# Expert weights split in place during the attention; the token table uses their memory first

## The chip, the cores and the metric

The kernel runs on one core of a Trainium2 chip. A core has TensorE (PE), VectorE (DVE), ScalarE (ACT), GpSimd (POOL) and SyncE (SP, which here only starts DMAs), and 16 DMA engines. Each engine runs its own list of instructions in order, and they wait for each other by semaphores. The metric is the device time in microseconds (us) of one execution.

## The reference

4096 tokens (16 sequences of 256) go through an embedding, six layers of linear attention and a mixture of experts. Width D is 256.

```python
h = take(W.T, x)                          # W: [256, 50257], ids below 12564
a = layernorm(h)
for l in range(6):
    t = layernorm(a) * gamma[l] + beta[l]
    q, k, v = split(t @ w_qkv[l])
    q = softmax(q, axis=1); k = softmax(k, axis=2)
    out = einsum('bic,bij->bjc', q, einsum('bic,bjc->bij', k, v))
    a = a + out @ w_out[l] + b_out[l]
h = h + a
x = layernorm(h)
# 8 experts, top 2 of x @ gate_w, weights by softmax of the two; and one shared expert
h = h + sum_e w_e * ((silu(x @ w1[e]) * (x @ w2[e])) @ w3[e]) + shared(x)
```

## The kernel before

Every product is made in float16 with each factor split in a high and a low part (high times high, high times low, low times high), so each weight is needed as two float16 tiles: high is the float32 value scaled by 64 and rounded, low is the difference that rounding left. An expert has 3072 float32 columns (w1 and w2 side by side, then w3); there are nine experts with the shared one.

Stages, in order of time:

1. **Table.** The ids need only the first columns of W, which lie the wrong way round. SP loads chunks of 512 columns into `VW` (four buffers), TensorE transposes them, ScalarE and VectorE copy one half each from PSUM to `VR`, ScalarE's queue stores them as rows to `emb_rows` in DRAM. A stretch is 7 steps of 4 chunks, 28 chunks; with these ids there is one stretch. SP loads the weights of experts 0 and 1 ahead of the first chunk and of 2 and 3 behind it, into two float32 buffers `FST` (1.57 MB an expert); `expert_high` (L911, L912, ScalarE) and `expert_low` (L1087, L1089, VectorE) split them.
2. **Gathers.** When all rows are stored, GpSimd issues 32 indirect DMAs (L544) into `X`. In this time SP loads the other five experts and the two engines split all that are left.
3. **First norm.** Per group of 8 tiles (four groups): VectorE takes statistics (L1116, L1119), GpSimd adds epsilon and takes the root (L566, L568), SP stores the gathered rows as `h0_rows` (L383) for a later addition, VectorE normalizes `X` in place (L1128) once store and root are done. GpSimd's `cut` (L561) makes the low parts of layer 0's weights between its roots; ScalarE makes the high ones (L941, L945). SP waits until all experts are split before it stages layer 0's weights.
4. **Attention.** 96 items (16 sequences, 6 layers), one turn each, as a software pipeline written out in `item_loop`. In turn t TensorE works at q and k of item t+2 and at m, p and the output of item t; VectorE normalizes item t+5 (L1156) and takes statistics of item t+6; GpSimd does gamma and beta, the bias and the split of item t+5 (L579 to L592) and the root of item t+6 (L596). VectorE and GpSimd start at turn -6 (`AHEAD`), the others at -2: turns -6 to -1 are called lead turns here. SP issues the transposes of h (L423) and of the exponent of q (L432). The turns of the first half of each layer (`prep`) also split a slice of the next layer's weights: ScalarE scales and rounds, GpSimd takes the difference (`cut`). ScalarE and GpSimd have nested loops for this, VectorE and TensorE one plain loop over pairs of turns.
5. **Feed-forward.** Gates, ranks, scattering of tokens to slots, the shared expert (16 pairs of tiles) and 39 pairs of slots of the eight experts. For each pair TensorE does two `up` halves (L809, 24 multiplies each) and a `down` (L825, 24). Which expert's weights a pair takes is read from a table, so the columns of these weights have a register in their address (`cols`, `which`).

Orders that matter for the change. VectorE in a turn: reciprocal of k's sums (L1169), the addition of item t-1 (L1163), low v (L1174), low m (L1178), maximum of q (L1183), maximum of k (L1186), low k (L1190), norm (L1156), low PR (L1196), statistics (L1200), low exponent of q (L1207), aggregates (L1213). TensorE's last four multiplies of an item (L759) wait for the low PR; the products m, q, k, p, v (L712) follow, twelve multiplies each. ScalarE in a turn: high v (L983), high m (L989), high k (L995), negated maximum of q (L999), exponents (L1004, L1009), high PR (L1014), exponents of k.

Of the kernel before, what the change touches and what calls it, by code (L numbers as in the profile page):

```python
# [17 lines left out]
def tower(nc, x_ids, tok_w, w_qkv, w_out, b_out, gamma, beta, gate_w, ew1, ew2, ew3, sw1, sw2, sw3, out):  # L18
# [37 lines left out]
    VBUF = 4  # L56
    VSTEP = VCH * VBUF
    VBLK = VCH // P
    STRETCH = 7
    VROWS = STRETCH * VSTEP  # L60
    NSTRETCH = -(-VOCAB // VROWS)
# [17 lines left out]
    with ctx:  # L79
# [8 lines left out]
        W12h = sb("W12h", [P, NE, KH, 2 * HID], f16)  # L88
        W12l = sb("W12l", [P, NE, KH, 2 * HID], f16)
        W3h = sb("W3h", [P, NE, HC, D], f16)  # L90
        W3l = sb("W3l", [P, NE, HC, D], f16)
# [11 lines left out]
        padt = sb("padt", [P, 2, ROW], f32)  # L103
# [17 lines left out]
        s_fstage = [sem(f"s_fstage{i}") for i in range(2)]  # L121
        s_fhi, s_flo = sem("s_fhi"), sem("s_flo")
        s_gath = [sem(f"s_gath{i}") for i in range(4)]
        s_h0st = [sem(f"s_h0st{i}") for i in range(4)]
        s_reuse, s_passed, s_passed_sp = sem("s_reuse"), sem("s_passed"), sem("s_passed_sp")
# [3 lines left out]
        NG4 = NT // 4  # L129

        emb = ExitStack()
        ident = sb("ident", [P, P], f32, emb)
        VW = [sb(f"VW{i}", [P, KH, VCH], f32, emb) for i in range(VBUF)]
        VR = [h0b[:, 0, :, :], h0b[:, 1, :, :]]
        VR += [sb(f"VR{i}", [P, VBLK, D], f32, emb) for i in range(2, VBUF)]
        FST = [sb(f"FST{i}", [P, KH * 2 * HID + HC * D], f32, emb) for i in range(2)]  # L140

        idrow = W3l[0:1, :, :, :].rearrange("p e c n -> p (e c n)").bitcast(i32)[:, 0:TOK]
        idmax = sb("idmax", [1, 1], i32, emb)
        emb.close()

        FW12 = KH * 2 * HID


# [7 lines left out]
        WSN = WL // WSL  # L156
        Wsc = sb("Wsc", [P, WSN], f32, att)
        Wn = sb("Wn", [P, 2, WL], f16, att)
        hhl = [sb(f"hhl{i}", [P, 2, TB, D], f16, att) for i in range(2)]
        rows = sb("rows", [P, 2, 3, D], f32, att)  # L160
# [16 lines left out]
        att.close()  # L177

# [128 lines left out]
        def item_loop(eng, one, lead, prepare=False, behind={}):  # L307

            def pair(h, prep):
                for p in range(2):  # L310
                    one(eng.snap(h * 2 + p), p, prep)

            for t in range(-lead, 2):
                one(t, t % 2, prepare and t >= 0)
            if not prepare:
                with eng.Fori(1, (ITEMS - AHEAD) // 2) as h:
                    pair(h, False)
# [12 lines left out]
            for t in range(ITEMS - AHEAD, ITEMS):  # L330
                one(t, t % 2, False)
                if t in behind:
                    behind[t]()
# [1068 lines left out]
```

## Time and profile before

| | us |
|---|---|
| median of 3 runs | 1513.89 |
| lowest and highest | 1504.29, 1516.38 |
| the profiled execution | 1518.33 |
| its span, first to last instruction | 1516.6 |

The engines' busy time in the stages of the profiled execution:

| stretch, us | what | PE | DVE | ACT | POOL | granted PE clock | DMA, GB/s |
|---|---|---|---|---|---|---|---|
| 0 to 96 | table | 43.92 | 30.26 | 23.95 | 2.31 | 0.75 | 365 |
| 96 to 154 | gathers | 0.00 | 30.52 | 19.64 | 42.35 | 0.50 | 276 |
| 154 to 195 | first norm, lead turns | 0.59 | 23.63 | 6.88 | 25.27 | 0.50 | 132 |
| 195 to 985 | attention | 765.67 | 680.29 | 596.48 | 685.07 | 0.99 | 79 |
| 985 to 1130 | attention's end, gates, shared expert | 117.48 | 81.24 | 75.44 | 81.41 | 0.94 | 113 |
| 1130 to 1517 | shared expert, experts | 355.48 | 182.51 | 109.31 | 135.47 | 0.98 | 64 |

How to read rows: a line of the timeline gives the start, the duration, the engine, the line in the code, the operation, what it writes and reads, the shape and the count; in brackets stands how long the engine had been idle and what ended that. Rows of the same kind that follow each other are merged, so a duration with x8 is that of eight instructions. Matmuls overlap, so their rows are longer than their distance. PEld is TensorE's load of weights. The clock is a share of 2.4 GHz.

### The profile page before, as it was taken

What the parts mean: (1) busy time and instruction counts of PE and PEld (TensorE: products, weight loads), DVE (VectorE), ACT (ScalarE), POOL (GpSimd) and SP (SyncE); (2) the same over time, 40 slices, a digit from 0 to 9 for tenths busy, and PEclk for the clock granted to TensorE, in tenths of its full rate; (3) what the DMA queues carried; (4) which work ended last, traced back from release to release, by engine and by line L of the source; (5) the groups of instructions that cost most, each with busy time, mean ns of one, the idle gap of its engine ahead of it and who ended that gap; (6) DMA issues with size and microseconds to landing.
All of it is one profiled execution on the core that took longest, in us unless ns stands there. A gap on an engine that the chain in (4) does not pass through costs nothing. (4 is left out here: it accounts for less than half of the span.)

```text
span 1516.6 us, 37800 instructions
## 1 busy us (share of the span) xinstructions
PE 1283.1 (85%) x11400; PEld 1096.8 (72%) x11401; DVE 1028.5 (68%) x2634; ACT 831.7 (55%) x2253; POOL 971.9 (64%) x967
## 2 busy tenths in 40 slices
PE   2620069999999999999999999877898999999996
PEld 2520058888888888888888888766787888888885
DVE  3235558888888888888888888765456444444443
ACT  2233148777877777787787777665442222222231
POOL 0037589888988988988888888647542333333333
PEclk8755589999999999999999999999999999999998
DMA  9998433253235235333523423684434343434340
GB/s 321 398 323 299 129 69 63 62 128 69 62 69 128 62 64 127 69 62 76 121 59 66 97 61 64 92 113 126 113 99 134 64 65 53 69 54 69 51 69 8
DMA packets 356716, 160.28 MB, mean 106 GB/s; under 512 B 283953, under 2 KB 340273, under 8 KB 356657
## 3 DMA queue, kind: packets, MB, share of 16 engines
q1 hardware_dynamic: 321810, 119.56, 33.7%
q0 software_dynamic: 20064, 25.32, 9.0%
q10 hardware_dynamic: 14784, 14.68, 2.7%
q8 instruction: 29, 0.48, 0.1%
q14 instruction: 29, 0.24, 0.0%
HBM read 46.08 MB, written 44.21 MB: 60 GB/s over the span
## 5 line engine op out<-in xcount | busy, mean ns | idle before, releaser
L712 PE MATMUL bank<-hT,Wc 128*128 128x256 f16 x2304 | 286.3, 275 | 110.5 <-DMA hT<-hhl 104.9
L712 PEld LDWEIGHTS bank<-hT,Wc 128*128 128x128 f16 x2304 | 226.8, 99 | 138.9 <-issue 111.3
L674 POOL DMA_INDIRECT out_rows<-h0b,payin x78 | 121.7, 1560 | 232.6 <-DVE h0b L1370 203.8
L809 PE MATMUL bank<-xTg,W12h 128*128 128x256 f16 x1248 | 187.2, 273 | 0.0
L579 POOL TENSOR_TENSOR h0b<-h0b,rows 128x512 f32<-128x512 f32 x96 | 122.0, 1270 | 94.0 <-issue 47.3
L1038 ACT ACTIVATE silu<-bank 128x512 f32<-128x512 f32 x110 | 65.5, 596 | 211.0 <-PE bank L809 205.2
L1311 DVE SCALAR_TENSOR_TENSOR gT<-bank,silu 128x512 f32<-128x512 f32 x110 | 76.0, 691 | 144.4 <-ACT silu L1038 142.0
L712 PE MATMUL bank<-Wc,MT 128*128 128x256 f16 x1152 | 142.3, 274 | 8.6 <-DVE MT L1178 8.6
L825 PE MATMUL bank<-W3h,gThl 128*128 (+1 forms) x880 | 127.5, 276 | 23.5 <-DVE gThl L1317 20.5
L712 PE MATMUL bank<-khl,eqT 128*128 128x256 f16 x1152 | 141.4, 272 | 5.7 <-issue 0.2
L712 PE MATMUL bank<-Wc,hT 128*128 128x256 f16 x1152 | 141.7, 273 | 0.0
L809 PEld LDWEIGHTS bank<-xTg,W12h 128*128 x1248 | 122.1, 98 | 14.2
L712 PEld LDWEIGHTS bank<-khl,eqT 128*128 128x128 f16 x1152 | 109.7, 98 | 28.9 <-issue 16.5
L1317 DVE TENSOR_TENSOR gThl<-gT,gThl 128x512 f16<-128x512 f32 x110 | 76.6, 696 | 78.1 <-ACT gThl L1042 73.1
L712 PEld LDWEIGHTS bank<-Wc,MT 128*128 128x128 f16 x1152 | 112.6, 98 | 23.1 <-DVE MT L1178 9.7
L1042 ACT ACTIVATE gThl<-gT 128x512 f16<-128x512 f32 x110 | 69.3, 630 | 98.2 <-DVE gT L1311 94.4
L1156 DVE TENSOR_SCALAR h0b<-X,amv,arstd 128x256 f32 (+1 forms) x192 | 79.1, 453 | 64.8 <-POOL arstd L596 64.8
L712 PEld LDWEIGHTS bank<-Wc,hT 128*128 128x128 f16 x1152 | 112.9, 98 | 13.3
L585 POOL TENSOR_TENSOR hhl<-h0b,rows 128x512 f16<-128x512 f32 x96 | 122.1, 1272 | 0.0
L586 POOL TENSOR_TENSOR h0b<-h0b,rows 128x512 f32<-128x512 f32 x96 | 122.0, 1270 | 0.0
L580 POOL TENSOR_TENSOR X<-X,rows (+2 forms) x96 | 121.9, 1270 | 0.0
L825 PEld LDWEIGHTS bank<-W3h,gThl 128*128 128x128 f16 x880 | 85.1, 98 | 49.2 <-issue 31.1
(153 smaller groups left out, 2941.3 us busy)
## 6 DMA issues: line engine op xcount, KB each, us to landing
VW<-in_L_tok_W SPq DMA_DIRECT2D x28, 512.0 KB, 6.3
FST<-in_L_ffn_ew SPq DMA_DIRECT2D x24, 512.0 KB
emb_rows<-h0b ACTq DMA_DIRECT2D x14, 512.0 KB, 8.2
emb_rows<-VR ACTq DMA_DIRECT2D x14, 512.0 KB, 9.4
Wc<-Wn SPq DMA_DIRECT2D x48, 128.0 KB, 2.2
Wst<-in_L_attn_w_qkv SPq DMA_DIRECT2D x6, 768.0 KB, 4.8
h_rows<-X SPq DMA_DIRECT2D x4, 1024.0 KB, 4.5
X<-h_rows POOLq DMA_DIRECT2D x8, 512.0 KB, 6.9
```

Source lines behind the costliest of these rows:

```text
L579: pool.tensor_tensor(xn[:, :, :], xn[:, :, :], row(0), ALU.mult).then_inc(s_hg, 1)
L580: pool.tensor_tensor(tiles(u), tiles(u), row(2), ALU.add).then_inc(s_xb, 1)
L585: pool.tensor_tensor(h_hi, xn[:, :, :], row(1), ALU.add)
L586: pool.tensor_tensor(hf[:, :, :], xn[:, :, :], row(1), ALU.add).then_inc(s_hf, 1)
L674: pool.indirect_dma_start(out=out_rows, out_offset=bass.IndirectOffsetOnAxis(ap=got(j % PAYS, w, 0, i32), axis=0), in_=yout[j % 2][:, w, : ...
L712: last = mm(to, lhs(a, k, o), moving, start=(i == 0 and k == 0), stop=(i == 2 and k == 1))
L809: last = mm(to, cols((W12h, W12l)[a], e, k, w * HID + (2 * half + c) * P, P), moving, start=(n_ == 0), stop=(n_ == 5))
L825: last = mm(pb[4 + p][:, w * D:(w + 1) * D], gThl[:, p, a, c, w * P:(w + 1) * P], cols((W3h, W3l)[b], e, c, 0, D), start=(n_ == 0), stop=( ...
L1042: A(gThl[:, p, 0, 2 * half:2 * half + 2, :], gT32[:, half, :, :], ACT.Copy).then_inc(s_ghi, 1)
L1156: last = V.tensor_scalar(xn[:, k, :], X[:, bass.ds(seq(w) * TB + k, 1), :].rearrange("p a n -> p (a n)"), amv[p][:, k, 0:1], arstd[p][:, k ...
L1311: V.scalar_tensor_tensor(gT32[:, half, :, :], pb[2 * half + 1][:, :].rearrange("p (c n) -> p c n", c=2), 1.0 / WS, silu[:, half, :, :], AL ...
L1317: V.tensor_tensor(gThl[:, p, 1, c, :], gT32[:, half, :, :], gThl[:, p, 0, c, :], ALU.subtract).then_inc(s_glo, 1)
```

## The change

- The nine experts' high and low parts are one float16 tile `Wall` (9 x 6144 columns), high and low alternating in chunks of 512 columns, 54 chunks in all. The same memory, seen as float32 (`Wf`), first holds the table's buffers, now five of each kind (`VBUF = 5`, a stretch is 5 steps of 5 chunks: 25 chunks), the ids, the identity, and the gathered rows `G`.
- Experts are loaded as float32 into `Wf`, one expert's width ahead of where their parts go, and split in place, one copy (ScalarE) and one difference (VectorE) of 512 columns a turn: 8 chunks ahead of the attention, 8 in the second half of each of the first five layers, the last 6 in turns 84 to 89. The shared expert comes into a buffer of its own (`lastf`) that overlays attention weights no longer needed.
- Experts 0 and 1 are loaded when the table is stored, 2 and 3 between the transposes of items 1 and 2, four more at the end of a layer each, the last at the start of the last layer.
- Rows are gathered into `G`, and the norm goes from `G` to `X`, so it does not wait for the store of `h0_rows`.
- Layer 0's weights are staged right behind the table's loads; their low parts are taken by VectorE. Only the first of GpSimd's four roots and of VectorE's four norms stands ahead of the lead turns: the other roots follow turns -6, -5, -4, the other norms turns -5, -3, -1.
- VectorE takes the nested loops too. The padding row is stored from one tile by a broadcast.

```diff
-    VBUF = 4
+    VBUF = 5
+    EXP = KH * 2 * HID + HC * D
+    XCH = HID
+    XPER = EXP // XCH
+    XALL = NE * XPER
+    XEARLY = NB // 2
-    STRETCH = 7
+    STRETCH = 5
...
+        PLAIN, CUT, EXPERT, LAST = range(4)
+        def item_loop(eng, one, lead, other=True, between={}):
...
+                with eng.Fori(1, quarter) as h:
+                    pair(h, CUT)
+                with eng.Fori(0, quarter) as b:
+                    pair(eng.snap(b + quarter), EXPERT, eng.snap(b + XEARLY // 2))
                 with eng.Fori(1, DEPTH - 1) as l:
+                    with eng.Fori(0, quarter) as b:
+                        pair(eng.snap(l * (2 * quarter) + b), CUT)
+                    with eng.Fori(0, quarter) as b:
+                        pair(eng.snap(l * (2 * quarter) + b + quarter), EXPERT, eng.snap(l * quarter + b + XEARLY // 2))
...
@@ sync
+            n = steps(sp)
+            with sp.Fori(1, n) as step:
...
+            stage(0)
+            stage_rows(0)
...
+            for j in range(VBUF):
+                sp.wait_ge(s_wst[j], n * 16)
+            for e in range(2):
+                load_expert(e)
             for j in range(4):
                 install(0, j)
             stage(1)
...
             turns(-4, 0)
             turns(-3, 1)
+            for e in range(2, 4):
+                load_expert(e)
+            stage_rows(1)
...
                     stage(l + 2)
                     stage_rows(l + 2)
+                if l + 4 < E:
+                    sp.wait_ge(s_xlo, NB // 2 * l + XEARLY + 1)
+                    load_expert(l + 4)
@@ gpsimd
+            first_root(0)
...
+            item_loop(pool, one, AHEAD, between={g - 7: partial(first_root, g) for g in range(1, 4)})
@@ tensor
+            def cols(a, e, chunk, c0, n):
+
+                return Wall[:, bass.ds(e * 2 * EXP + (chunk * 2 + a) * XCH + c0, n)] if isinstance(e, int) else \
+                    Wall[:, bass.ds(e + ((chunk * 2 + a) * XCH + c0), n)]
@@ scalar, def one, behind the high part of k
+                if c is not None:
+                    act.wait_ge(s_xload, 48 * (NE if kind == LAST else layer(t) + 4))
+                    act.sem_inc(s_passed, 1)
+                    act.wait_ge(s_xlo, c)
+                    act.sem_inc(s_passed, 1)
+                    expert_high(c, staged_last(c) if kind == LAST else staged(c))
@@ vector
+            def expert_low(n, from_):
+
+                dve.wait_ge(s_xhi, n + 1)
+                V.scalar_tensor_tensor(Wall[:, bass.ds(n * (2 * XCH) + XCH, XCH)], from_, WS,
+                                       Wall[:, bass.ds(n * (2 * XCH), XCH)], ALU.mult, ALU.subtract).then_inc(s_xlo, 1)
...
+            def first_norm(g):
                 dve.wait_ge(s_rstd, g + 1)
                 for t in range(8 * g, 8 * g + 8):
+                    last = V.tensor_scalar(X[:, t, :], G[:, t, :], mv[:, t, 0:1], rstd[:, t:t + 1], ALU.subtract, ALU.mult)
...
+            for n_ in range(XEARLY):
+                expert_low(n_, staged(n_))
...
+            for g in range(4):
+                first_stats(g)
+            first_norm(0)
...
                     last.then_inc(s_klo, 1)
+                if c is not None:
+                    expert_low(c, staged_last(c) if kind == LAST else staged(c))
                 if have(t + 5):
                     norm(t + 5, 1 - p)
...
+            item_loop(dve, one, AHEAD, between={**{2 * g - 7: partial(first_norm, g) for g in range(1, 4)},
+                                                **{ITEMS - 5 + g: partial(stats_of, g) for g in range(5)}})
```

## Rows read from the trace of the kernel before

**Rows 1.** Stretch, length; busy PE, PEld, DVE, ACT, POOL; clock, DMA share, GB/s.
```profile
625.00:697.00 72.00, 70.62 (x633) 60.40 (x632) 62.92 (x156) 57.17 (x182) 64.18 (x69) 1.00 0.30 62
```

**Rows 2.** Same columns, ten microseconds of the table phase.
```profile
74.00:84.00 10.00, 5.90 (x25) 4.79 (x26) 2.77 (x4) 2.39 (x4) 0.00 (x0) 0.53 1.07 396
```

**Rows 3.** Timeline (start us, us, engine, line, operation [idle before]) of the gathers.
```profile
99.65 2.50 POOL L544 DMA_INDIRECT X<-emb_rows,idx  x1 [96.32 <-issue]
...
112.23 2.29 DVE L1087 SCALAR_TENSOR_TENSOR W12l<-FST,W12h 128x2048 f16<-128x2048 f32 x1 [6.74 <-ACT W3h L912]
...
113.45 1.95 POOL L544 DMA_INDIRECT X<-emb_rows,idx  x1 [0.30 <-issue]
...
149.87 1.01 POOL L544 DMA_INDIRECT X<-emb_rows,idx  x1 [0.30 <-issue]
```

**Rows 4.** Timeline, from the last gather to the first attention turn.
```profile
153.02 0.32 POOL L552 TENSOR_SCALAR idx<-idx 128x32 int32<-128x32 int32 x1 [2.14 <-DMA X<-emb_rows,idx]
...
155.87 2.67 DVE L1128 TENSOR_SCALAR X<-X,mv,rstd 128x256 f32<-128x256 f32 x8 [4.52 <-POOL rstd L568]
...
158.46 2.70 DVE L1116 BATCH_NORM_STATS2 stats<-X 128x6 f32<-128x256 f32 x8
...
175.45 3.29 DVE L1128 TENSOR_SCALAR X<-X,mv,rstd 128x256 f32<-128x256 f32 x8 [3.08 <-POOL rstd L568]
...
179.81 0.76 DVE L1200 BATCH_NORM_STATS2 stats<-X 128x6 f32<-128x256 f32 x2
```

**Rows 5.** Timeline, GpSimd in two lead turns, and the first maximum of q.
```profile
182.84 1.26 POOL L579 TENSOR_TENSOR h0b<-h0b,rows 128x512 f32<-128x512 f32 x1 [0.94 <-issue]
...
190.62 1.26 POOL L579 TENSOR_TENSOR h0b<-h0b,rows 128x512 f32<-128x512 f32 x1 [0.94 <-issue]
...
199.11 0.66 DVE L1183 TENSOR_REDUCE qmax<-bank 128x2 f32<-128x512 f32 x1
```

**Rows 6.** Timeline of one turn in the middle of the attention.
```profile
553.86 0.20 ACT L999 ACTIVATE nqmax<-qmax 128x2 f32<-128x2 f32 x1 [0.81 <-DVE qmax L1183]
...
554.71 0.87 DVE L1190 SCALAR_TENSOR_TENSOR khl<-bank,rzks,khl 128x256 f16<-128x256 f32 x2
...
555.35 0.71 POOL L596 TENSOR_TENSOR arstd<-avar,mhalf 128x2 f32<-128x2 f32 x1
...
556.09 0.74 DVE L1156 TENSOR_SCALAR h0b<-X,amv,arstd 128x256 f32 x2 [0.51 <-POOL arstd L596]
...
556.74 0.69 DVE L1196 SCALAR_TENSOR_TENSOR PR<-bank,PR 128x512 f16<-128x512 f32 x1
...
557.48 0.61 PE L759 MATMUL bank<-PR,vT 128*128 128x256 f16 x4
...
559.54 1.47 PE L712 MATMUL bank<-hT,Wc 128*128 128x256 f16 x12
...
560.85 1.47 PE L712 MATMUL bank<-Wc,hT 128*128 128x256 f16 x12
```

**Rows 7.** Timeline of the feed-forward, VectorE's difference beside GpSimd's.
```profile
1101.84 0.69 DVE L1317 TENSOR_TENSOR gThl<-gT,gThl 128x512 f16<-128x512 f32 x1 [0.70 <-ACT gThl L1042]
...
1104.95 2.13 POOL L627 TENSOR_TENSOR xrow<-h0b,xrow 128x1024 f16<-128x1024 f32 x1 [4.65 <-ACT xrow L976]
...
1106.77 0.85 DVE L1317 TENSOR_TENSOR gThl<-gT,gThl 128x512 f16<-128x512 f32 x1 [0.69 <-ACT gThl L1042]
```

**Rows 8.** Timeline, maxima of q in every second turn, fourth layer.
```profile
659.63 0.68 DVE L1183 TENSOR_REDUCE qmax<-bank 128x2 f32<-128x512 f32 x1
...
676.24 0.68 DVE L1183 TENSOR_REDUCE qmax<-bank 128x2 f32<-128x512 f32 x1
...
692.47 0.68 DVE L1183 TENSOR_REDUCE qmax<-bank 128x2 f32<-128x512 f32 x1
```

**Rows 9.** Timeline, TensorE in a down product of the feed-forward.
```profile
1298.36 0.65 PE L825 MATMUL bank<-W3h,gThl 128*128 x4 [0.39 <-DVE gThl L1317]
...
1298.85 0.60 PE L825 MATMUL bank<-W3l,gThl 128*128 x4
```

More of the change, by code:

```diff
@@ L305, in tower, with pair, hook @@
         AHEAD = 6
-        def item_loop(eng, one, lead, prepare=False, behind={}):
-            def pair(h, prep):
+        PLAIN, CUT, EXPERT, LAST = range(4)
+        def item_loop(eng, one, lead, other=True, between={}):
+            def pair(h, kind, c=None):
                 for p in range(2):
-                    one(eng.snap(h * 2 + p), p, prep)
+                    one(eng.snap(h * 2 + p), p, kind, None if c is None else eng.snap(c * 2 + p))
+            def hook(t):
+                if t in between:
+                    between[t]()
+            quarter = NB // 4
@@ L439, in turns @@
                     turn_eq(t + 2 if isinstance(t, int) else sp.snap(t + 2), p)
-            stage(0)
-            stage_rows(0)
+            for j in range(VBUF):
+                sp.wait_ge(s_wst[j], n * 16)
+            for e in range(2):
+                load_expert(e)
             for j in range(4):
@@ L542, in _ @@
                 pool.sem_inc(s_passed, 1)
[L543 to L547 removed]
+                for g in range(4):
+                    gather(g)
                 for g in range(4):
@@ L715, in _, with one @@
             blk = lambda o: slice(o * P, (o + 1) * P)
-            def one(t, p, prep):
+            def one(t, p, kind, c):
                 u = t + 2
@@ L1025, in one @@
                     A(zks[:, :], zk[:, :], ACT.Copy, scale=1.0 / KS).then_inc(s_zks, 1)
-                if prep:
+                if kind == CUT:
                     l = layer(t) + 1
                     cut(t + WSL if isinstance(t, int) else act.snap(WSL * l + t % WSL), l, t % WSL)
-            item_loop(act, one, 2, prepare=True, behind={ITEMS - 4: lambda: high(0), ITEMS - 2: lambda: high(1)})
+            item_loop(act, one, 2, between={ITEMS - 4: lambda: high(0), ITEMS - 2: lambda: high(1)})
             def gate(i, p, half):
@@ L1140, in _ @@
             dve.wait_ge(s_route, 2)
+            for g in range(4):
+                first_stats(g)
+            first_norm(0)
             def stats_of(g):
@@ L1214, in one @@
                     last.then_inc(s_amv, 1)
-            item_loop(dve, one, AHEAD, behind={ITEMS - 5 + g: partial(stats_of, g) for g in range(5)})
+            item_loop(dve, one, AHEAD, between={**{2 * g - 7: partial(first_norm, g) for g in range(1, 4)},
+                                                **{ITEMS - 5 + g: partial(stats_of, g) for g in range(5)}})
             add(ITEMS - 1)
```

250 lines of the change are left out of this document (110 added, 140 removed).

## The prediction, made before the change was run

> **What bounds the kernel now.** I read the stage table first (busy time by stretches), then ten-microsecond stretches of the table phase, then the timeline of the gathers, of the stretch up to the first attention turn, and of one turn in the middle of the attention.
>
> From 195 us on TensorE is the bound: in a steady attention stretch it is busy 70.6 of 72 us at a granted clock of 1.00 (2.4 GHz) [rows 1]. Up to 195 us nothing is bound by compute. First the table phase: 28 chunks of 512 columns go in and out (2 x 0.524 MB each) and four experts' weights are loaded beside them; the DMA engines are full at 396 GB/s [rows 2]. Then 32 gathers are issued by GpSimd from 99.65 to 150.88 us, one per 1.31 us (1.01 and 0.30 idle) where nothing disturbs them [rows 3]. Then, from 153.02 to 179.81 us, four groups of root, norm and weight cut run one after another before the first attention turn starts its statistics [rows 4]. From that mark the rest is one chain, so a microsecond saved before it is saved at the end.
>
> **The change, part by part.**
>
> *Table phase.* Before: 28 chunks are 29.4 MB, twelve expert arrays of 0.524 MB are 6.3 MB. After: stretches of 5 steps of 5 chunks, 25 chunks, 26.2 MB, no expert. 9.4 MB less at 396 GB/s [rows 2] is 23.8 us. I give back 2 us, an estimate: the five first loads land together, and a new load waits for a transpose, so the queues run dry once near 10 us. Gathers start at 99.65 - 21.8 = 77.9. Bounds: 17 to 24 us.
>
> *Gathers.* They take 51.2 us against 32 x 1.31 = 41.9. The other 9.3 us is stalls of this kind: the 2.29 us difference of 2048 elements runs on VectorE from 112.23 to 114.52, and the gather begun at 113.45 ends at 115.40, which is 0.88 after the difference ended [rows 3]. Seven such pairs of differences (2.29 and 1.22 us) stand in this stretch, so 38% of their time became stall. After, eight expert differences of 0.69 [rows 7] and eight small cuts of about 0.35 fall here: 8.3 us, of which 30% is 2.5. Gathers take 44.4, 6.8 less. Bounds 41.9 and 50.2. The Trainium skill (SBUF — State Buffer, Who interferes with whom) says that a VectorE instruction with two SBUF inputs contends with a GpSimd one that reads SBUF, and that descriptor writing needs the other half of the port. The rows do not contradict it if it is the gather's start, which reads indices, that waits; if nothing waited, the gathers would take 41.9 and the sum would be 2.5 us lower.
>
> *Roots, norms and cuts.* Layer 0's cuts move to VectorE under the gathers, where it waits anyway, as do the early eight expert chunks on ScalarE and VectorE. The norm no longer waits for the store of h0. After the last gather only two things remain ahead of turn -6: statistics of the last group (2.70 and about 0.7 for its aggregates) and the norm of the first (2.67), 6.1 us; the root (153.02 to 155.87) runs beside the statistics [rows 4]. 26.8 becomes 6.1: -20.7.
>
> Mark of the first turn: 179.81 - 21.8 - 6.8 - 20.7 = 130.5, -49.3.
>
> *Lead turns.* Three roots (about 2.0 us each: 0.3 and 1.7 within the 2.85 of [rows 4]) now stand on GpSimd behind turns -6, -5, -4. GpSimd paces these turns, 7.78 us from one to the next, and idles 0.94 in each for the norm [rows 5], so a root costs 2.0 - 0.94, three 3.2. Norms of groups 1 to 3 (24 instructions of about 0.33) stand on VectorE among GpSimd's 1.27 us operations. How they collide shows in the old norms: 2.67 where GpSimd worked at a root, 3.29 beside a cut [rows 4]. I take 3 us (bounds 0 and 24 x 0.33 = 8). Experts 2 and 3 are loaded in SP's queue between the transposes of items 1 and 2: 3.1 MB at 396 GB/s is 7.9 us in a turn of about 8.8; 1 us. Queued behind it are the first transposes of h and of q, which TensorE waits for. Together +7.
>
> *Expert chunks in 46 turns* (40 in second halves of layers, 6 in the last). ScalarE's copy, about 0.6 us, is put ahead of the negated maximum, where it idles 0.81 [rows 6]: nothing, but it would cost up to 0.6 without that gap. VectorE's difference is 0.69 undisturbed [rows 7], between the low part of k and the norm. There the low part ends at 555.58 and the norm starts at 556.09, since GpSimd's root ends at 556.06 [rows 6]: 0.51 of cover. With 0.69 and one more wait (0.05, estimated) the norm starts 0.23 later. Behind it stand the low part of PR (556.74 to 557.43) and TensorE's four multiplies that wait for it (557.48), then m, q and k, whose maximum and low part lead back to the norm. This ring has no other slack, so each turn is 0.23 longer: 46 x 0.23 = +10.6. Bounds: 0 (all in the idle time) and 0.69 x 46 = 32.
>
> *Nested loops on VectorE.* It takes the nested loops that ScalarE and GpSimd already had. A pair of turns with cuts takes 16.61, one without 16.23 [rows 8], so extra sequencer work costs tenths at most; VectorE's own hides behind its 0.69 and 0.24 us operations at the turn's end. 0, bound 40 pairs x 0.38 = 15.
>
> *Expert loads in the layers* (five of 1.57 MB, four of them behind the weight stage, at 396 GB/s 4.0 us of DMA each [rows 2]). The next transposes queue behind them; TensorE uses those nearly a turn later. +1, bound 5 x 4 = 20.
>
> *Feed-forward.* Same multiplies, but twice as many register offsets, since high and low parts alternate in one tile. At a down product, four multiplies with new offsets take 0.65 where four with old ones take 0.60 [rows 9]. Four more such in each of 39 pairs: 39 x 0.05 = +2, bound 5.
>
> **Sum.** -49.3 + 7 + 10.6 + 0 + 1 + 2 = -28.7. The span 1516.6 becomes 1487.9. The profiled execution took 1518.3, 4.4 above the median of 1513.89; against the median the sum gives 1485.2.
>
> **Rivals.**
>
> *A. As summed*, within some 10 us: 1485.
>
> *B. TensorE hides it all.* Its own work in a turn is 7.86 us (72 multiplies of 0.109; the twelve multiplies of one product start 1.31 apart), under the 8.1 of the steady turn. If the 10.6 vanishes and the lead turns cost 3: 1513.9 - 49.3 + 3 + 3 = 1470.6. Against it: the ring above, where TensorE already waits for PR's low part.
>
> *C. The difference isn't covered at all.* VectorE reads both inputs from SBUF, as in the feed-forward, where such a difference takes 0.69 alone and 0.85 when begun 0.31 before the end of a GpSimd operation [rows 7]: it waits for that operation. In the turn it meets GpSimd's root, which ends at 556.06 [rows 6]. Then the norm starts at 556.06 + 0.69, 0.66 late: 46 x 0.66 = 30.4 instead of 10.6, 1513.9 - 28.7 + 19.8 = 1505, within 1%. For it: 0.85. Against: a root of 1.7 us did not lengthen the eight norms beside it (2.67) [rows 4]. The Trainium skill (SBUF — State Buffer, Who interferes with whom) has this as an exclusive lock for the whole instruction; by that rule this case holds.
>
> *D. The table phase is bound by its buffers' round trip, not by bytes.* Then 3 chunks of about 3.0 us and the 7 us of experts ahead of the first chunk go, 16 instead of 21.8: 1491. Against it: the DMA engines' busy share of 1.07 at 396 GB/s [rows 2].
>
> *E. Slower.* The difference arrives in the turn while GpSimd's longer operation (1.16 to 1.27 us) runs, waits for its end, and pushes back the next one on GpSimd, whose root the norm needs. One such meeting costs up to 1.27 + 0.69 - 0.51 = 1.45 per turn, 46 x 1.45 = 67: 1513.9 - 39.3 + 67 = 1541. It turns the sign from 39.3 / 46 = 0.85 us per turn. Against it: the norm holds GpSimd back in every turn, so GpSimd is at its root or idle when the difference comes [rows 6].
>
> **Chances.** A 0.60, B 0.10, C 0.17, D 0.08, E 0.05. I take 1% (15 us) as about what a measurement of this kernel can tell from no change. A, B, D are faster by more than that: 0.78. C falls within 1% with most of its chance: 0.16. Slower: 0.06. The time is that of A, 1485; the range runs from 1467 (B, with the gathers at their floor) to 1504 (next to C).
>
> **What the profile after would show.** Gathers start near 78, end near 122; the first turn's statistics near 130; the first maximum of q near 152 (199.11 before [rows 5]); pairs of turns with expert chunks near 16.7 against 16.23, pairs with cuts as before at 16.6; feed-forward longer by 2. Wrong would be: a gather start above 84 (D), pairs with expert chunks at 17.5 (C) or above 18 (E), VectorE's difference longer than 0.7 in those turns, or more than 12 us lost between the first maximum of q and turn 0.

## The result, and the profile after

| | before | after |
|---|---|---|
| median of 20 runs each, us | 1509.65 (1504.29 to 1516.38) | 1504.12 (1499.55 to 1509.61) |
| ratio | | 0.996, 95% interval 0.9945 to 0.9975 |
| the profiled execution, us | 1518.33, span 1516.6 | 1501.22, span 1499.3 |

The change brings 5.5 us, 0.4%, where 29 were forecast (a ratio of 0.981). It is less than the 1% that the prediction took as no change, and 1504.12 stands just past the upper end of the range, 1504, where rival C was expected; but C is not what happened.

The same marks in both profiles tell where the time went. "q(n)" is the start of the maximum of q of item n, so six layers are q(0) to q(95). "First gate" is ScalarE's table load ahead of its first silu, and "thirtieth half" is its thirtieth silu; the shared expert has 32 of them.

| us | before | after | difference | forecast |
|---|---|---|---|---|
| gathers start | 99.6 | 81.3 | -18.3 | -21.8 |
| first gather to first statistics of turn -6 | 80.2 | 50.5 | -29.7 | -27.5 |
| from there to q(0) | 19.3 | 29.0 | +9.7 | lead turns, in all +7 |
| layer 0, q(0) to q(16) | 132.6 | 135.1 | +2.5 | chunks +1.8, part of the lead turns |
| layers 1 to 4, q(16) to q(80) | 524.2 | 550.0 | +25.8 | chunks +7.4, loads +1 |
| layer 5, q(80) to q(95) | 126.5 | 128.5 | +2.0 | chunks +1.4 |
| q(95) to the first gate | 20.6 | 20.9 | +0.3 | 0 |
| gates and shared expert, to the thirtieth half | 157.8 | 146.2 | -11.6 | 0 |
| from there to the end | 355.8 | 357.8 | +2.0 | +2 |

The differences add up to -17.3, the difference of the two spans. The medians differ by 5.5 only. The row of -11.6 fits this gap: the change alters nothing in that stretch but the addresses of its weights, and over all kernels of this document it takes from 146 to 161 us (below). The profiled execution of before, 8.7 above its median of 20, had it long; that of after, 2.9 under its median, had it short. Without it -5.7 is left.

One row spoils the forecast: layers 1 to 4. Their turns are alike (7.9 to 8.6 us from one maximum of q to the next) but for one in each layer, the second, which takes 14.09, 15.28, 14.51 and 14.16 us after and 8.23 to 8.26 before. These four are +25.0. Some of it comes back two turns later (8.09 to 8.11 us where before has 8.60 to 8.61), and a kernel without the long turns (the first experiment) takes 527.7 us for the four layers. So the long turns cost 22.3 of the 25.8, net, and the chunks 3.5.

Stretches of the profile after, in the form of [rows 1]: the steady attention is as before, 70.64 us of TensorE in 72. The second fence has the turn before a long one, the first 14.1 us of the long one of layer 2 (it runs from 441.40 to 456.68), and the 8 us behind those.

```profile
core 0: us, PE busy (x) PEld busy (x) DVE busy (x) ACT busy (x) POOL busy (x), PEclk, DMA share, GB/s
625.00:697.00 72.00, 70.64 (x632) 60.41 (x630) 65.38 (x160) 58.05 (x183) 63.01 (x67) 1.00 0.32 62
```

```profile
433.40:441.40 8.00, 8.00 (x75) 6.97 (x74) 7.61 (x21) 6.48 (x21) 6.54 (x8) 1.00 0.73 201
441.40:455.50 14.10, 9.33 (x64) 7.20 (x62) 7.16 (x18) 5.36 (x18) 9.86 (x11) 0.76 0.75 204
455.50:463.50 8.00, 8.00 (x76) 7.15 (x74) 6.96 (x18) 6.69 (x22) 3.43 (x3) 1.00 0.18 35
```

TensorE, VectorE and ScalarE each do about one turn's work in nearly twice the time, so it is a wait for something else. The timeline of that turn after (SPq are SP's DMA issues):

```profile
435.55 0.43 SPq L390 DMA_DIRECT2D Wall<-in_L_ffn_ew  x1
436.02 0.47 SPq L391 DMA_DIRECT2D Wall<-in_L_ffn_ew  x1
436.89 1.80 SPq L392 DMA_DIRECT2D Wall<-in_L_ffn_ew  x1
438.89 3.36 SPq L414 DMA_TRANSPOSE hT<-hhl  x1
442.44 3.76 SPq L423 DMA_TRANSPOSE eqT<-EQhl  x1
448.24 0.84 ACT L1031 ACTIVATE EQhl<-bank,nqmax 128x256 f16<-128x256 f32 x2 [4.87 <-DMA eqT<-EQhl]
449.60 0.69 DVE L1227 SCALAR_TENSOR_TENSOR PR<-bank,PR 128x512 f16<-128x512 f32 x1 [4.45 <-ACT PR L1036]
449.71 1.87 PE L766 MATMUL bank<-PR,vT 128*128 128x256 f16 x8 [4.77 <-ACT PR L1036]
452.22 2.76 PE L722 MATMUL bank<-khl,eqT 128*128 128x256 f16 x12
```

And the DMA issues of 438.5 to 443.2 in the same trace, us from issue to landing in the last column:

```profile
hT<-hhl SPq DMA_TRANSPOSE x1, 8.4
eqT<-EQhl SPq DMA_TRANSPOSE x1, 5.8
```

The reader is to see a chain. From 432.93 SP issues the next layer's weight stage (1.4 MB) and right behind it the expert's 1.57 MB. The transposes stand behind those 3 MB: the issue of one takes 3.36 and 3.76 us instead of 1.24, and the landing of h's 8.4 instead of 3.1. `EQhl` has one buffer, so ScalarE may not write the next exponent before the transpose has read the last; it stands 4.87 us at L1031. The high part of PR, its next instruction, is late, and VectorE and TensorE wait 4.45 and 4.77 for it. Then the granted clock has fallen: the stretch has 0.76, and eight multiplies take 1.87 instead of 1.04, twelve 2.76 instead of 1.47, which is the rate of 1.2 GHz.

### The profile page after: what moved, and what is told of

Read it like the earlier page. It is cut to its first block and busy times, and to the rows that moved or that the text cites. A ratio compares the mean times of both kernels' runs of the same rounds, so it can differ in the third digit from the quotient of the medians.

```text
span 1499.3 us, 38135 instructions
## 1 busy us (share of the span) xinstructions
PE 1285.4 (86%) x11376; PEld 1098.3 (73%) x11377; DVE 1044.4 (70%) x2675; ACT 831.6 (55%) x2286; POOL 960.6 (64%) x958
## 5 line engine op out<-in xcount | busy, mean ns | idle before, releaser
L819 PE MATMUL bank<-xTg,Wall 128*128 128x256 f16 x1872 | 210.9, 273 | 0.0
L819 PEld LDWEIGHTS bank<-xTg,Wall 128*128 x1872 | 183.1, 98 | 21.3
L835 PE MATMUL bank<-Wall,gThl 128*128 (+1 forms) x1320 | 160.2, 276 | 23.8 <-DVE gThl L1348 23.8
L835 PEld LDWEIGHTS bank<-Wall,gThl 128*128 128x128 f16 x1320 | 125.1, 98 | 57.3 <-issue 26.8
L722 PE MATMUL bank<-khl,eqT 128*128 128x256 f16 x1152 | 144.7, 276 | 5.1 <-DVE khl L1219 0.3
L766 PE MATMUL bank<-PR,vT 128*128 128x256 f16 x768 | 103.6, 280 | 21.4 <-ACT PR L1036 21.2
```

The lines of the kernel that those rows point to most:

```text
L722: last = mm(to, lhs(a, k, o), moving, start=(i == 0 and k == 0), stop=(i == 2 and k == 1))
L766: mm(o_ps[:, o, :], vT[p][:, a, k, blk(o)], PR[:, 0, k, :], start=(o == 0 and a == 0 and k == 0), stop=False)
L819: last = mm(to, cols(a, e, 2 * k + w, (2 * half + c) * P, P), moving, start=(n_ == 0), stop=(n_ == 5))
L835: last = mm(pb[4 + p][:, w * D:(w + 1) * D], gThl[:, p, a, c, w * P:(w + 1) * P], cols(b, e, KH * 2 + c // 2, c % 2 * D, D), start=(n_ == ...
```

## The experiments

The experiments ran on three chips. The kernel before took 1509.61 (median of 19) on the first chip, 1522.71 (19) on the second and 1521.72 (7) on the third, so kernels of different chips are compared by their ratio to before alone. Unless a diff says otherwise each kernel is the changed one plus its edit.

**The burst spread over three turns, first chip.** The three arrays of an expert go out one a turn, in the first turns of layers 1 to 4, not behind the weight stage.

```diff
-                if l + 4 < E:
-                    sp.wait_ge(s_xlo, NB // 2 * l + XEARLY + 1)
-                    load_expert(l + 4)
...
+                if 1 <= l < DEPTH - 1:
+                    sp.wait_ge(s_xlo, NB // 2 * (l - 1) + XEARLY + 1)
+                    for n_ in range(4):
+                        turns(first + n_, n_ % 2)
+                        if n_ < 3:
+                            load_expert(l + 3, (n_,))
```

> The changed kernel, but the experts that are loaded at the end of layers 0 to 3 (1.57 MB each, right behind the 1.4 MB of the weight stage and its rows) are loaded one array of 0.52 MB a turn in the first three turns of the next layer. Theory Q (queueing): in the changed kernel the transposes behind the 3 MB block land 8.4 and 5.8 us after their issue, ScalarE may not write the exponent of q into its only buffer until the transpose has read it, and the turn takes 14.1 to 15.3 us instead of 8.1. Then all four long turns vanish: about 4 x 6.3 = 25 us less than the changed kernel, near 1479. Rival N (nested loops and the instruction fetches at the change from one loop to the next cost it, since the long turns stand at the seam of two layers): the four long turns stay, no gain. The prediction's term was 1 us for all of these loads.

1479.04 us (4 runs), ratio 0.9793 (0.9753 to 0.9832). Layers 1 to 4 take 132.4, 131.8, 131.7, 131.8 instead of 137 to 138; the second turn takes 8.24 to 8.33. The same place in its timeline and its DMA issues:

```profile
431.89 1.26 SPq L417 DMA_TRANSPOSE hT<-hhl  x1
434.07 1.74 SPq L426 DMA_TRANSPOSE eqT<-EQhl  x1
```

```profile
hT<-hhl SPq DMA_TRANSPOSE x1, 5.2
eqT<-EQhl SPq DMA_TRANSPOSE x1, 3.8
```

The same bytes are loaded and the long turns are gone: 25.1 us by the medians, 22.3 between q(16) and q(80) in the profiles. The interval of the ratio leaves the median's figure some 6 us of room either way; the profiles' is the finer one. A weight stage alone delays the transposes by 2.1 and 0.8 us, and that costs nothing.

**The bytes taken away, same chip.** The four loads keep their place and number, but bring 16 columns an array. Experts 4 to 7 are computed from other weights here, and 2 MB of weights are loaded into their place during the gathers.

```diff
-                    load_expert(l + 4)
+                    load_tiny(l + 4)
```

> The changed kernel with the same four loads shrunk to three arrays of 16 columns a piece, from the gate's weights, in their old place; the experts 4 to 7 are thus computed with wrong weights (2 MB of others fill their memory during the gathers). Theory Q: if only the placing of the bytes costs, this gains as much as spreading them (25 us); if the bytes themselves cost something wherever they are, this is faster than the spread loads by that. Rival N: no gain.

1480.72 (4 runs), ratio 0.9799 (0.976 to 0.9839), with q(95) at 952.5 as in the kernel before this one. So it is neither the wait on `s_xlo` nor the number of issues, but the bytes in one burst; and spreading gives back all that they cost in the layers. Whether the transposes were late because they stood behind the burst in SP's queue, or because the burst filled the 16 DMA engines, is not separated: no run put it in another engine's queue.

**A second buffer for the exponent's halves, third chip.** The burst stays; only what it stalls is changed.

```diff
-        EQhl = sb("EQhl", [P, 2, KH, SEQ], f16, att)
+        EQhl = [h0b[:, 1, 0:2, :].rearrange("p a d -> p (a d)").bitcast(f16)
+                .rearrange("p (a k n) -> p a k n", a=2, k=KH),
+                sb("EQhl", [P, 2, KH, SEQ], f16, att)]
...
-                    if not (isinstance(u, int) and u < 1):
-                        act.wait_ge(s_eqT[1 - p], landed(u - 1))
+                    if not (isinstance(u, int) and u < 2):
+                        act.wait_ge(s_eqT[p], landed(u - 2))
```

> The changed kernel with a second buffer for the exponent's two halves (EQhl), so that ScalarE writes the next exponent without waiting until the last one has been read by its transposition; the second buffer is a part of h0b that is free during the layers. The bursts of expert weights at the ends of the layers stay. It asks through what the late transpositions stall the turn. Theory 1, the single buffer carries part of the stall (in the changed kernel's long turn ScalarE waits 4.87 us at the second exponent for the transposition's landing, and VectorE and TensorE wait 4.45 and 4.77 behind it): the long turns fall from 14.1 to 15.3 us to some 11, layers 1 to 4 from 137 to about 134 each, in all 12 to 16 us, 1489 to 1493 where the changed kernel has 1504.1 (ratio to before 0.986 to 0.989). Theory 2, TensorE has to have the same transpositions in any case and the buffer only shows their lateness: long turns as before, ratio 0.995 to 0.997. In both the ordinary turns stay 8.1 to 8.25.

1500.39 (4 runs), ratio 0.9849 (0.982 to 0.9879). The long turns take 11.28, 10.74, 10.34 and 10.34 us: 15.3 of 25.0 are gone with the burst in place, and layers 1 to 4 take 535.6 instead of 550.0. The same place in its timeline:

```profile
438.16 3.90 SPq L415 DMA_TRANSPOSE hT<-hhl  x1
442.25 3.65 SPq L424 DMA_TRANSPOSE eqT<-h0b  x1
442.48 0.84 ACT L1034 ACTIVATE EQhl<-bank,nqmax 128x256 f16<-128x256 f32 x2
448.18 1.47 PE L723 MATMUL bank<-khl,eqT 128*128 128x256 f16 x12 [2.56 <-DMA eqT<-h0b]
```

The transposes are as late as in the changed kernel, but ScalarE goes on at once. What is left of a long turn, 2.1 to 3.0 us, goes with TensorE's own wait for the transpose, 2.56 in the turn shown; twelve multiplies behind it still take 1.47. So of the 6.3 us of a burst about 2.4 come through TensorE's wait and 3.8 through the single buffer, with what follows from it. The first theory had it at 12 to 16 us; it is 14.4 over the four layers.

**Norms all ahead of the lead turns, first chip.** The four roots and the four norms stand ahead of turn -6.

```diff
-            first_norm(0)
+            for g in range(4):
+                first_norm(g)
```

> The changed kernel with all four roots and norms ahead of the lead turns, as in the kernel before (but still from the gathered rows). In the changed kernel a norm of eight tiles takes 7.4, 7.5 and 6.5 us in the lead turns beside GpSimd's long operations, 2.7 elsewhere, and the first maximum of q waits behind one of them. Theory P (VectorE is blocked by GpSimd): the three norms take 2.7 each, the first turn starts 8 us later, the first maximum of q comes 19.3 behind it as in the kernel before instead of 29.0: the sum is a gain of 1 to 4 us. Rival: the 29.0 comes of the roots and the two experts' load, then the norms cost their 8 us on the path and give little back: 5 us slower.

1504.96 (10 runs), ratio 0.9965 (0.9941 to 0.999): as the changed kernel. Turn -6 starts at 140.2 instead of 131.8, q(0) comes 19.3 behind it, as in before. The 32 norm instructions take 10.44 us, 0.33 each. What weaving saved ahead of the mark (8.4) it lost behind it (9.7 at q(0)). Roots and norms moved together here, so this run alone does not tell the one from the other; the next does.

The timeline of the changed kernel shows why. The second group of eight norms, and GpSimd beside it:

```profile
135.83 1.27 POOL L588 TENSOR_TENSOR h0b<-h0b,rows 128x512 f32<-128x512 f32 x1
135.90 7.42 DVE L1151 TENSOR_SCALAR X<-Wall,mv,rstd 128x256 f32<-128x256 f32 x8 [0.29 <-POOL rstd L570]
137.05 1.31 POOL L589 TENSOR_TENSOR X<-X,rows 128x512 f32<-128x512 f32 x1
138.33 1.30 POOL L594 TENSOR_TENSOR hhl<-h0b,rows 128x512 f16<-128x512 f32 x1
139.60 1.30 POOL L595 TENSOR_TENSOR h0b<-h0b,rows 128x512 f32<-128x512 f32 x1
141.06 1.15 POOL L601 TENSOR_TENSOR hhl<-h0b,hhl 128x512 f16<-128x512 f32 x1
160.78 0.68 DVE L1212 TENSOR_REDUCE qmax<-bank 128x2 f32<-128x512 f32 x1
```

Eight norms take 7.42 us, where the first group took 2.64; the next groups take 7.49 and 6.50. The single records inside that row start at 135.90, 137.17, 138.44, 139.71 and 140.97, each some 0.1 behind the start of a GpSimd operation, and last 1.34 to 1.39; the last three last 0.40, which is also the record of a norm alone (0.33 from start to start). One norm instruction passes for each GpSimd operation, and GpSimd loses 0.04. The maximum of q(0), whose product was done some 12 us earlier, stands behind the second such group.

**Norms of groups 1 to 3 on ScalarE, first chip.** GpSimd makes minus mean times root for it; ScalarE idles here.

```diff
+            act_norm(1)
+            item_loop(act, one, 2, between={-2: lambda: act_norm(2), -1: lambda: act_norm(3), ...})
...
+                    last = A(X[:, t, :], G[:, t, :], ACT.Identity, bias=nm0[:, t:t + 1], scale=rstd[:, t:t + 1])
```

> The changed kernel with the norms of groups 1 to 3 on ScalarE (x times root minus mean times root, two small operations more on GpSimd for each root), the first ahead of its turns, the others behind its turns -2 and -1. Theory P: ScalarE is not blocked by GpSimd, a norm of eight tiles takes 2.5 to 3 us there, and the first maximum of q comes about 20 to 22 us behind the first turn instead of 29.0; with the later norm's 6.5 us gone too, 8 to 12 us less than the changed kernel. Rival: no gain, the pace of the lead turns is GpSimd's and it has 0.5 us more per root.

1502.29 (10 runs), ratio 0.9938 (0.9918 to 0.9959), 1.8 us under the changed kernel, within the uncertainty. Eight norms beside GpSimd take ScalarE 4.04, and q(0) comes 23.0 behind the mark instead of 29.0, but layer 0 takes 1.8 more. With roots and norms both ahead it came 19.3 behind: 6.0 of the 9.7 go with VectorE's norms, and 3.7 are left with the roots, now with two operations more each, behind the lead turns. From its timeline:

```profile
136.79 1.26 POOL L595 TENSOR_TENSOR h0b<-h0b,rows 128x512 f32<-128x512 f32 x1
136.86 4.04 ACT L1063 ACTIVATE X<-Wall,nm,rstd 128x256 f32<-128x256 f32 x8 [37.82 <-POOL nm L577]
146.55 1.27 POOL L595 TENSOR_TENSOR h0b<-h0b,rows 128x512 f32<-128x512 f32 x1
153.48 0.74 DVE L1201 TENSOR_SCALAR h0b<-X,amv,arstd 128x256 f32<-128x256 f32 x2 [8.09 <-POOL arstd L612]
```

GpSimd sets the pace now, 9.76 us from one lead turn to the next, with the root and the two new instructions in it; VectorE waits 8.09 for its root. The collision is shown. Of 5.7 us gained at q(0) 4.7 are left at q(95) in the profiles (969.7 against 974.4), and less in the medians; the first theory had 8 to 12 in all.

**Layer 0's stage behind the table, second chip.** The stage, gate weights and padding rows are issued after the last store.

> The changed kernel, but layer 0's weights, its rows, the gate's weights and the padding rows (1.7 MB) are loaded and stored once the table is stored, not between the table's last loads and its last stores. The prediction's table phase was counted in bytes and left these 1.7 MB out; the gathers started at 81.3 where it said 77.9. Theory B (the phase is bound by bytes): 1.7 MB at 396 GB/s is 4.3 us, gathers start near 77, all else follows, 3 to 4 us less than the changed kernel. Rival L (by the last stores' own latency): gathers start where they did, no gain.

1513.12 (10 runs), ratio 0.9936 (0.9918 to 0.9954). The gathers start at 76.1 instead of 81.3 and turn -6 at 128.5, q(0) at 157.5: 3.3 us arrive at q(0).

**Experts 2 and 3 loaded ahead of the gathers' end, with the burst spread, second chip.**

> The kernel with spread loads, and experts 2 and 3 loaded together with 0 and 1 during the gathers instead of between the transposes of items 1 and 2. Theory Q: the transposes of h of item 2 and of q of item 0 (7.5 and 4.1 us to landing) fall back to 3.1, the turns of 14.0 and 10.0 us shrink to about 9, 5 to 7 us less than with spread loads alone. Rival: the long turns come from the norm that blocks VectorE for 6.5 us (its wait was seen at the low part of m), then at most 1 us.

1493.69 (4 runs), ratio 0.9811 (0.9775 to 0.9847), the same as with the spread burst alone (0.9793). The two long turns of layer 0 go from 14.01 and 10.04 in the spread kernel to 13.46 and 9.28: beside the woven norms the loads cost 1.3 us, not the 5 to 7 of the first theory. The norms do not explain all the rest. With the norms ahead and the loads in place the second turn still takes 11.72 (8.59 before), and ScalarE waits 4.39 us there for the transpose of the exponent. The two delays overlap, and taking one away leaves the other.

**The expert chunk's difference made twice in every turn, second chip.**

```diff
+                    V.scalar_tensor_tensor(scr[:, :], src_, WS,
+                                           Wall[:, bass.ds(c * (2 * XCH), XCH)], ALU.mult, ALU.subtract)
```

> The changed kernel with a second difference of 512 columns, into a scratch tile, ahead of VectorE's difference in each of the 46 turns with an expert chunk. The first one lengthened a pair of turns by about 0.1 us where the prediction said 0.46. Theory S (the first one used up the cover of about 0.5 us, and the ring over TensorE, VectorE's chain and back has no other slack): each turn grows by 0.6 to 0.67, a pair with expert chunks from 16.27 to about 17.6, in all 46 x 0.64 = 29 us more than the changed kernel. Rival T (VectorE's difference is taken out of slack that TensorE's pace leaves, and there is more): clearly less, 0.2 a turn, 10 us.

1536.25 (6 runs), ratio 1.0082 (1.0055 to 1.0109). Turns with chunks take 8.55 and 8.85 instead of 7.95 and 8.26, +0.60 each for an instruction whose record is 0.68 long. In 46 turns that is 28 us; by the ratios the kernel is some 18 us over the changed one, and by the profiles outside the gates and the shared expert 22. The rest comes back in and around the long turns, two of which are 13.35 and 13.44 us here. From its timeline:

```profile
558.83 0.68 DVE L1225 SCALAR_TENSOR_TENSOR scr<-Wall 128x512 f16 x1
559.42 0.68 DVE L1110 SCALAR_TENSOR_TENSOR Wall<-Wall  x1
560.03 0.73 DVE L1186 TENSOR_SCALAR h0b<-X,amv,arstd 128x256 f32 x2
```

So the turn is set by a ring through VectorE, as the prediction had it: the second difference has no cover left at all. The first has nearly all of it. In the timeline of the changed kernel:

```profile
556.82 0.87 DVE L1219 SCALAR_TENSOR_TENSOR khl<-bank,rzks,khl 128x256 f16<-128x256 f32 x2
557.15 0.71 POOL L605 TENSOR_TENSOR arstd<-avar,mhalf 128x2 f32<-128x2 f32 x1
557.60 0.68 DVE L1109 SCALAR_TENSOR_TENSOR Wall<-Wall  x1
558.20 0.73 DVE L1185 TENSOR_SCALAR h0b<-X,amv,arstd 128x256 f32 x2
559.58 0.33 PEld L770 LDWEIGHTS bank<-PR,vT 128*128 128x128 f16 x4 [0.20 <-DVE PR L1227]
```

From the start of low k to the start of the norm it is 1.38 us in this turn and was 1.38 before too (554.71 to 556.09 in [rows 6]). Records of instructions that follow one another on VectorE overlap, by 0.09 and 0.08 here, which the sum had not counted, and GpSimd's root ends 1.04 behind the start of low k, where it was 1.35, so it doesn't hold the norm any more.

**Four edits together, second chip** (spread burst, stage behind the table, norms on ScalarE, experts 2 and 3 early).

> All in one: expert loads spread over three turns, layer 0's stage behind the table, norms of groups 1 to 3 on ScalarE, experts 2 and 3 loaded with 0 and 1 during the gathers. By adding up: spread loads 25, stage 4, norms on ScalarE 2 to 5, experts 2 and 3 out of the lead turns 6 to 8 (turns 1 and 2 take 14.0 and 10.0 there instead of 8 to 9): about 38 to 42 us less than the changed kernel, near 1464. If the lead turns' loss is the norms' alone, the last item gives nothing: near 1471.

1485.83 (6 runs), ratio 0.9751 (0.9723 to 0.9779), worse than the sum of its parts. Turn -6 started only at 133.7, 16.2 behind the start of the last gather instead of 8.6.

**The same without the early experts, third chip.**

> Three of the earlier edits without the fourth: expert loads spread over three turns, the first layer's staging behind the table, groups 1 to 3 of the first norm on ScalarE; experts 2 and 3 are loaded behind the gathers again, not before them. In the combination of four the first turn's mark stood 16.1 us behind the last gather instead of 8.6 to 9.8, with seven differences of those experts on VectorE ahead of the gathers' statistics. Theory 1, those differences delay the statistics: the mark returns to 128.5, the first q maximum comes 23 us behind at 151.5 (156.6 in the combination of four), layer 0 takes 136, the whole 3.5 to 5 us less than the combination of four: ratio to before 0.972 to 0.973. Theory 2, the delay is of another origin (stores, GpSimd's queue): mark at 133, ratio 0.975 or more.

1481.45 (4 runs), ratio 0.9726 (0.9697 to 0.9755). The mark is at 128.1, q(0) at 151.1, 23.0 behind. The early experts' differences had stood ahead of the gathers' statistics on VectorE: shown by the mark. The ratio alone would not tell it, its interval overlaps the last one's. Layer 0 takes 137.8 here, so of the 5.6 us at the mark 3.0 arrive at q(16) (288.9 against 291.9).

**Three edits and the second exponent buffer, third chip.**

> The three parts and the second exponent buffer together. Where the bursts are gone the buffer has little left to carry. Theory 1 (the single buffer matters only when transpositions land late): as the three parts alone within 0.002 of ratio, layers 1 to 4 131.4 to 131.8 each. Theory 2 (in every turn ScalarE waits a little at that buffer and the turn is set by it): ordinary turns fall from 8.2 by 0.1 or more, layers by 1.5 or more each, ratio lower by 0.005 or more.

1479.05 (4 runs), ratio 0.9721 (0.9699 to 0.9743). Layers 1 to 4 take 131.4 each, 131.4 to 131.5 without the buffer, as the first theory has it; layer 0 takes 135.2 instead of 137.8. Layer 0 is where experts 2 and 3 are loaded between transposes, and with them loaded early it took 135.2 without the buffer too (four edits together). By these single profiles the two experts in one block stalled that layer at the same buffer. The kernel is the fastest by ratio, 2.8% under before and, by the ratios, 2.4% under the changed kernel; from the one without the buffer the ratio doesn't tell it.

**The kernel before once more, third chip.**

> The kernel before once more, with a profile, for how far a stretch that no edit touches differs from execution to execution: the stretch from the first gate product to the twentieth dynamic half (gates, shared expert, lists), which took 157.8 us in the first profile of before and 146.2 to 159.6 in those of the changed kernel and its variants. Theory 1 (it varies by itself): the layers agree with the first profile within 0.5 us each and this stretch may differ by up to 13. Theory 2 (it is a property of the kernel before): 157 to 159 again.

1520.29, span 1518.5. The layers agree with the first profile within 0.3 us each. The stretch of gates and shared expert takes 160.7. It took 157.8 and 146.2 in the profiles of before and after that the forecast was compared by, 146.5 to 146.6 in three kernels on the first chip and 151.9 in the fourth, and 159.3 to 160.7 in all eight on the other two, whose runs of before are 12 to 13 us longer too. Stretches of two profiles, first before on the third chip, then the changed kernel:

```profile
1003.60:1060.00 56.40, 42.07 (x432) 34.85 (x431) 34.18 (x164) 31.02 (x44) 37.35 (x43) 0.88 0.67 120
1060.00:1164.30 104.30, 91.35 (x913) 78.01 (x912) 56.82 (x205) 45.24 (x69) 49.71 (x46) 0.97 0.39 113
```

```profile
995.30:1052.00 56.70, 45.44 (x492) 38.85 (x490) 36.37 (x168) 35.65 (x52) 37.90 (x42) 0.91 0.63 124
1052.00:1141.50 89.50, 81.27 (x856) 71.90 (x854) 55.88 (x202) 40.28 (x62) 50.03 (x47) 1.00 0.45 129
```

The work is nearly the same. The first stretches are about equally long (56.4 us at a granted clock of 0.88, 56.7 at 0.91); the second takes 104.3 us at 0.97 and 89.5 at 1.00. Whether the clock is the cause or follows from longer waits between the products these rows don't settle. That before can have it both long and short on one chip isn't shown either; its 20 runs spread over 12 us, as it would make them. The second theory (a property of before) falls with the eight, seven of which are other kernels.

## Why the prediction was wrong

*Table phase, forecast -21.8, measured -18.3.* Within the bounds of 17 to 24. The bytes were counted right for chunks and experts, but layer 0's stage, gate weights and padding rows, some 1.7 MB, now stand between the last loads and the last stores. With them behind the table the gathers start at 76.1 on another chip; 77.9 was forecast.

*Gathers, forecast 44.4 long, measured 42.9* from the start of the first (81.34) to the end of the last. Two of the 32 are stretched, beside six differences in a row. The timeline of after, VectorE and GpSimd:

```profile
95.91 3.70 DVE L1109 SCALAR_TENSOR_TENSOR Wall<-Wall 128x512 f16<-128x512 f32 x6 [9.25 <-ACT Wall L950]
96.04 1.45 POOL L546 DMA_INDIRECT Wall<-emb_rows,idx  x1 [0.30 <-issue]
97.79 1.50 POOL L546 DMA_INDIRECT Wall<-emb_rows,idx  x1 [0.30 <-issue]
99.59 1.01 POOL L546 DMA_INDIRECT Wall<-emb_rows,idx  x1 [0.30 <-issue]
```

They end at 97.49 and 99.29, inside the six differences, which end at 99.61: each is held for part of them, 0.4 to 0.5 us, and 0.9 us are lost in all, where the forecast put 30% of 8.3. Its own rows gave 38%, so its price was too high either way.

*Roots, norms, cuts: mark forecast at 130.5, measured 131.8.* Of -49.3, -48.0 came. This part, the largest, was right.

*Lead turns, forecast +7, measured +11.5* (9.7 to q(0), and 1.8 of layer 0's 2.5). The price of the woven norms was taken at 3 from two rows in which GpSimd did a root or a cut [rows 4], with a bound of 8. Beside the four operations with 512 columns it is 7.42 + 7.49 + 6.50 - 3 x 2.64 = 13.5 of VectorE's time, of which 6.0 arrive at q(0). The other 3.7 at q(0) are near the 3.2 forecast for the roots. The nearest row was not near: what GpSimd did beside the norm was another kind of work. The Trainium skill (SBUF — State Buffer, Who interferes with whom) counts tensor_scalar among the operations that can take the shared port pair and says that then the other engine fully blocks. The trace agrees: a norm starts 0.1 behind a GpSimd operation and ends behind that one's end, a record of 1.34 instead of 0.40, and GpSimd, which came first, takes 1.30 instead of 1.27.

*Expert chunks, forecast +10.6 for 46 turns, measured about +5.* In the spread kernel, which differs from the changed one in the burst alone, layers 1 to 4 take 3.5 more than before; the second half of layer 0 takes 0.7 more and the six chunk turns of layer 5 48.3 us against 47.6. Where the norms of groups 1 to 3 stand on ScalarE, layers 1 to 4 take 131.4 to 131.5 each against 131.0 and the sum is about +3: every second chunk turn is 8.26 there and 8.32 with the norms on VectorE, though those norms are done long before these turns. Why isn't shown. A pair of turns with chunks takes 16.21 to 16.28, where 16.7 was forecast and [rows 8] have 16.23 without (16.18 in before's other pairs behind it). The ring was right (twice the difference, +0.60 a turn), the cover was mis-sized: 0.51 was read as the gap between the end of one record and the start of the next, and what the difference adds is not its record of 0.69 but its pitch, 0.60 (557.60 to 558.20). So rival C, the price of 0.66 a turn, falls: GpSimd's root ran beside low k, and the difference of 0.68 was not longer than alone. E falls with it.

*Nested loops, forecast 0.* Pairs with cuts take 16.56 to 16.58 against 16.58 to 16.61. Right.

*Expert loads in the layers, forecast +1, bound 20, measured +22.3 (the four long turns themselves +25.0).* This is the step that failed. It said: "The next transposes queue behind them; TensorE uses those nearly a turn later." The first half is right in that they land late. The second looked at one user of the transposes. Their source is held too: ScalarE waits for the landing at L1031 before it overwrites `EQhl`, a wait that costs nothing while a transpose lands in 3 us. It was not asked what size of burst in that queue uses up the slack. 1.4 MB before did not (transposes 5.0 and 3.8), nor 1.57 MB alone at the start of layer 5 (its first turns take 7.91 to 8.32 us); 3 MB did. The bound of 20 was made from the bytes' own time, 4 us each, and left out what a stall sets off: the issue that blocks, the wait of three engines, the clock. That bound alone would have brought the sum to 1504, the end of the range, with nothing left for another miss. With the measured +5 for the chunks and +11.5 for the lead turns the sum without the burst is -48.0 + 11.5 + 5 + 2, or 29.5 us off before, near the 28.7 forecast. The profile of the spread kernel has 27.6 outside the gates and the shared expert; the medians have 30.6 (1509.61 to 1479.04), with whatever that stretch took in them. That the rest of the sum came so near is in part luck: the lead turns were 4.5 too low, the chunks 5.6 too high.

*Feed-forward, forecast +2, measured +2.0* (357.8 against 355.8), or +3.6 against the second profile of before (354.2). Within its bound of 5; no run separates the register offsets from the rest.

*Rivals.* B (TensorE hides it all) was half right, for the chunks. D gives 83.7 for the start of the gathers by its 16 us and the measured start of 81.3 lies between it and A; the run with the stage behind the table speaks for A. Of the prediction's signs of being wrong for C, D and E none appeared; there was no sign named for the term that failed. That the outcome landed where C was forecast is chance.

## What to carry to other kernels

Before a load is put in a queue that also carries small transfers on the path, ask how many bytes the queue then holds at once, and follow each delayed transfer to both ends: who waits for what it writes, and who waits to overwrite what it reads. The same bytes, split over three turns, made no turn long here. A cover between two instructions on one engine is measured start to start, and a price taken from a row is good only if the other engines do the same work beside it.

## What the runs showed of the hardware

- SP's issue of a transpose took 3.36 to 3.90 us behind 3 MB in its queue, 1.24 without, up to 1.74 in the spread kernel; the landing of h's took 8.4, 5.0 and 3.1 us behind 3 MB, 1.4 MB and nothing.
- VectorE's norm (one f32 input in SBUF, two per-partition scalars) goes in step with GpSimd's operations of 512 columns, one per operation: records of 1.34 to 1.39 instead of 0.40 us. GpSimd's take 1.30 instead of 1.27. Eight such norms on ScalarE, beside the same operations, took 4.04.
- In the changed kernel a stall of 4.77 us in TensorE's work was followed by multiplies at half rate (twelve in 2.76 us instead of 1.47, granted clock 0.50 from 449.6 to 454.0 us); behind one of 2.56 in the kernel with two exponent buffers the twelve took 1.47 at a clock of 1.00.
- The kernel before is 12 to 13 us longer on two of three chips. In the profiles of its variants one stretch of 150 us differs by as much between the chips (146.2 to 151.9 against 159.3 to 160.7); for before itself this isn't shown.
